# Multi-head attention by 32-row lanes in a two-layer attention and expert kernel

## The reference, cut to what matters

```python
# H = 16 heads, KPH = 4, LAT = 64, D = 128, S = 128 tokens
Q = (hs @ q_w + q_b).reshape(B, S, H, HD)     # only the first 4 of 8 columns are used
K = (hs @ k_w + k_b).reshape(B, S, H, KPH)
V = (hs @ v_w + v_b).reshape(B, S, H, KPH)
scores = einsum('bhsk,bhtk->bhst', Q[..., :KPH], K) / sqrt(KPH)
attn = softmax(scores)
ao = einsum('bhst,bhtv->bhsv', attn, V)
mla_out = concat([ao, 0]) @ o_w + o_b
# router: top 2 of 8 experts; each expert gelu(mla_out @ w1 + b1) @ w2 + b2
x = x + hs + 0.3 * moe_out                    # hs is the layer norm of x
```

## Time and profile before

| | us |
|---|---|
| median of 3 runs | 165.32 |
| lowest and highest | 164.41, 166.72 |
| the profiled execution | 164.66 |
| its span | 162.9 |

### The profile page before, as it was taken

One profiled execution on the slowest core, in us unless ns is written; L12 is line 12 of the kernel. 1 busy time (PEld: TensorE's weight loads), 2 busy tenths in 40 slices (PEclk: granted clock), 3 DMA queues, 4 the chain that ended last, 5 costly groups with the idle time before them and its releaser, 6 DMA issues.

```text
span 162.9 us, 3982 instructions
## 1 busy us (share of the span) xinstructions
PE 150.5 (92%) x1318; PEld 120.5 (74%) x1318; DVE 110.8 (68%) x408; ACT 108.3 (67%) x238; POOL 40.9 (25%) x122
## 2 busy tenths in 40 slices
PE   7998876999999999899999999999899999999891
PEld 5688755465545657457899899998799969779780
DVE  2866999879706767782228856986745897587744
ACT  8776972666785669689768743656953795666480
POOL 7698105221200294660000000220141200410100
PEclk9999997799999999999999999999999999999999
DMA  3538605217488113000100000000000000000022
GB/s 114 136 95 272 168 0 97 73 30 159 115 166 224 21 33 63 5 0 8 34 0 0 4 0 0 0 4 0 2 4 0 0 2 4 0 0 2 4 64 64
DMA packets 11071, 8.02 MB, mean 49 GB/s; under 512 B 1867, under 2 KB 10155, under 8 KB 11051
## 3 DMA queue, kind: packets, MB, share of 16 engines
q1 hardware_dynamic: 11051, 7.76, 19.5%
HBM read 5.26 MB, written 1.70 MB: 43 GB/s over the span
## 4 chain that ended last, share of the span: by engine, by line
PE 41%; issue 20%; DVE 10%; DMA 8%; ACT 7%; SPq 6%; POOL 5%; ACTq 1%; POOLq 1%; DVEq 0%
PE ps L1078 39%; DVE nmax L862 3%; DMA qbd<-scratch_q 3%; DMA w1s<-w1s 3%; DMA scratch_k<-part 2%; POOL rstd L563 2%; SPq L420 1%; ACT qbd L591 1%; SPq L371 1%; DVE qbd L856 1%; PE ps L1100 1%; POOL xn L557 1%; SPq L389 1%; ACTq L55 1%; ACT L714 1%
## 5 line engine op out<-in xcount | busy, mean ns | idle before, releaser
L699 ACT ACTIVATE vpad<-ps,b1o 128x256 f32<-128x256 f32 (+1 forms) x48 | 23.8, 545 | 16.7 <-PE ps L1078 16.6
L1078 PE MATMUL ps<-w2s,vpad 128*128 128x128 f32 x256 | 31.7, 276 | 0.2 <-DVE vpad L975 0.2
L1078 PEld LDWEIGHTS ps<-w2s,vpad 128*128 128x128 f32 x256 | 30.0, 192 | 0.8 <-issue 0.5
L862 DVE TENSOR_REDUCE nmax<-ps 128x4 f32<-128x512 f32 x32 | 21.0, 683 | 7.7 <-PE ps L1078 7.6
L975 DVE SCALAR_TENSOR_TENSOR vpad<-ps,comb,vpad 128x128 f32<-128x128 f32 x64 | 18.4, 342 | 8.6 <-PE ps L1078 8.6
L649 ACT ACTIVATE pexp<-ps 128x512 f32<-128x512 f32 x32 | 18.5, 596 | 6.1 <-PE ps L1078 5.9
L563 POOL TENSOR_TENSOR rstd<-veps,power 128x2 f32<-128x2 f32 (+1 forms) x6 | 4.8, 808 | 59.7 <-DVE veps L776 59.7
L1078 PE MATMUL ps<-ao,w_lo 128*128 128x256 f32 (+1 forms) x48 | 16.5, 358 | 0.3 <-ACT vpad L699 0.3
L1078 PE MATMUL ps<-ao,w_hi 128*128 128x256 f32 (+1 forms) x48 | 14.5, 317 | 0.0
L1078 PE MATMUL ps<-kst,qbd 128*128 128x128 bf16 x128 | 11.7, 225 | 1.4 <-DVE nmax L862 1.3
L1078 PEld LDWEIGHTS ps<-kst,qbd 128*128 128x128 bf16 x128 | 8.8, 101 | 5.7 <-issue 4.0
(11 more groups left out here) (224 smaller groups left out, 324.6 us busy)
## 6 DMA issues: line engine op xcount, KB each, us to landing
w1s<-in_L_ffn_w_dram SPq DMA_DIRECT2D x1, 1024.0 KB, 5.4
w1s<-w1s SPq DMA_DIRECT2D x8, 64.0 KB
kst<-scratch_k SPq DMA_DIRECT2D x4, 96.0 KB
qbd<-scratch_q SPq DMA_DIRECT2D x4, 96.0 KB
x<-in_x_dram SPq DMA_DIRECT2D x2, 128.0 KB, 2.4
x<-in_x_dram SPq DMA_DIRECT2D x1, 256.0 KB, 2.9
wqv<-in_L_xattn_W_qv_dram SPq DMA_DIRECT2D x1, 256.0 KB, 4.6
f1s<-in_L_ffn_W_dram SPq DMA_DIRECT2D x1, 256.0 KB, 5.0
```

Of the source, the lines that this page charges most:

```text
L699: act.activation(hT[:, k % 2, c, 0:n], ps[:, h1_bank(k, c), 0:n], ACT.Gelu, bias=b1o[:, e, c:c + 1]).then_inc(s["gelu_ok"], 1)
L862: dve.tensor_reduce(nmax[:, b, g, :], ps[:, n % 2, :].rearrange("p (j t) -> p j t", t=S), axis=AX.X, op=ALU.max, negate=True).then_inc(s[" ...
L1078: return nc.tensor.matmul(dst, lhsT, rhs, start=start, stop=stop)
```

## The change

Queries are no longer block-diagonal. `qst` holds them like the keys, one tile of [128, 4, 512] a half. A step of s1 and s2 is now a lane instead of a group: its four products contract over the 32 rows of one lane (`tile_position` (32 j, 0)), one for each group, 128 columns each. In each lane, 8 of the 32 rows are spare. The keys hold ones there, and the queries zeros. `mT` makes a second copy of the queries in PSUM (one product of 512 columns against the unit matrix) and adds to it the transposed maxima, which land in three of the spare rows; ScalarE copies this to `qm`, and s2 is then a single product a head. `selg`, its mask and the tile `mT` go. As an `av` step takes one group of all four lanes, it now needs all four exponentials of its sequence; `pexp` has seven slots.

Zeroing: `z_q` on POOL writes ones and zeros into `kst` and `qst` (4 memsets in all); `a_q` (four) and `a_k` on ScalarE go, and so do the waits for them in `parts`. `rows` makes two PSUM banks of keys, copied by ScalarE, and two of queries, copied by VectorE (2 copies instead of 16 behind ScalarE's). `gT` gets a tile of its own. The plan is a new one; FRONT stays at 2, 2 and 4.

```diff
+        qst = [sb(f"qst{i}", [P, GROUPS, T], BF16) for i in range(NHALF)]
+        qm = sb("qm", [P, 2, GROUPS, S], BF16)
+        pexp = sb("pexp", [P, SLOTS, GROUPS * S])
...
-                if h:
-                    sp.wait_ge(s["zero_q1"], GROUPS)
-                    sp.wait_ge(s["zero_k"], 1)
-                else:
-                    sp.wait_ge(s["zero_q"], u + 1)
-                    sp.wait_ge(s["qbd_ok"], GROUPS)
+                sp.wait_ge(s["zero_q"], u)
...
-                    sp.dma_start(qbd[h][rows_, :, j, d], sq).then_inc(s[f"stack_in{u}"], 16)
+                    sp.dma_start(qst[h][rows_, :, d], sq).then_inc(s[f"stack_in{u}"], 16)
...
+            def spare_rows(h):
+
+                half = slice(0 if h else T // 2, T)
+                pool.memset(kst[h][:, :, half].bitcast(FP32), PAIR_OF_ONES)
+                pool.memset(qst[h][:, :, half].bitcast(U32), 0).then_inc(s["zero_q"], 1)
...
-                for j in range(LANES):
-                    r = slice(ROWS * j, ROWS * (j + 1))
-                    last = dve.tensor_copy(qbd[0][r, g, j, 0:FRONT[0][1] * S], kst[0][r, g, T // 2:T])
-                last.then_inc(s["qbd_ok"], 1)
+                dve.wait_ge(s["rows_ps"], i + 1)
+                dve.tensor_copy(qst[0][:, 2 * i - 4:2 * i - 2, 0:T // 2],
+                                ps[:, ROW_BANKS[i], :].rearrange("p (g t) -> p g t", g=2)).then_inc(s["q0_ok"], 1)
...
-                for j in range(LANES):
-                    last = mm(ps[:, n % 2, j * S:(j + 1) * S], qbd[h][:, g, j, cols_of(b)], kst[h][:, g, cols_of(b)])
+                for g in range(GROUPS):
+                    last = mm(ps[:, n % 2, g * S:(g + 1) * S], qst[h][lane(j), g, cols_of(b)], kst[h][lane(j), g, cols_of(b)],
+                              tile=(ROWS * j, 0))
...
-                for j in range(LANES):
-                    last = mm(ps[0:MROWS, 7, j * S:(j + 1) * S], msp[:, b % 2, MROWS * j:MROWS * (j + 1)], identb[:, :])
+                mm(ps[:, 7, :].rearrange("p (g q) -> p g q", g=GROUPS), identb[:, :], qst[b // HALF][:, :, cols_of(b)], True, False)
+                for g in range(GROUPS):
+                    last = mm(ps[:, 7, g * S:(g + 1) * S], msp[:, b % 2, g, :], identb[:, :], False, g == GROUPS - 1)
...
-                mm(dst, kst[h][:, g, cols_of(b)], qbd[h][:, g, :, cols_of(b)], True, False)
-                mm(dst, selg[:, g, :], mT[:, b % 2, :, :], False, True).then_inc(s["s2_ps"], 1)
+                for g in range(GROUPS):
+                    last = mm(ps[:, 2 + n % 2, g * S:(g + 1) * S], kst[h][lane(j), g, cols_of(b)], qm[lane(j), b % 2, g, :],
+                              tile=(ROWS * j, 0))
+                last.then_inc(s["s2_ps"], 1)
...
-                pe.wait_ge(s["p_ok"], n + 1)
+                pe.wait_ge(s["p_ok"], LANES * (b + 1))
```

More of the change, by code:

```diff
@@ L1076, in _, with mm @@
         def _(pe):
-            def mm(dst, lhsT, rhs, start=True, stop=True):
-                return nc.tensor.matmul(dst, lhsT, rhs, start=start, stop=stop)
+            def mm(dst, lhsT, rhs, start=True, stop=True, tile=None):
+                return nc.tensor.matmul(dst, lhsT, rhs, start=start, stop=stop, tile_position=tile)
             def warm(n):
```

201 lines of the change are left out of this document (92 added, 109 removed).

## The result

The changed kernel takes 168.66 us (median of 4, 167.81 to 169.98), beside 164.87 us (4 runs, 164.32 to 166.72) of the kernel before on the same chip: ratio 1.022, 95% interval 1.011 to 1.033. Taken once more, beside e11, it was 169.91 us (4 runs, 168.91 to 170.59) against 165.43: 1.028, 1.021 to 1.035. By the mark of 2% the first ratio alone leaves it open whether this is slower, since its interval reaches under 1.02; the second says slower. The loss is some 4 us (3.8 and 4.5), where 165.0 and no difference had been forecast; the range, 161.2 to 169.0, holds the first median and not the second. The profiled execution took 168.47 us with a span of 166.6.

A forecast was written before the change was run, and what follows sets the result against it. TensorE was taken to bound attention's second part, behind a 13.8 us copy chain: attention to 47.9 + 27.2 = 75.1, plus expert layers 87.5 gives 162.6 of span, plus 2.4 makes 165.0 us; range 161.2 to 169.0.

The forecast's parts named there:

- rival C: TensorE's 3.2 us wait for the copies drops the clock to 1.2 GHz; 3 us lose 1.5: 166.5 us; chance 0.15.
- The front: Before sequence 4: fewer VectorE copies let the third split end at 34.1 instead of 36.2, 2.1 us gained, bounds 1.0 and 3.0.
- The copies: Third unit's chain from split to sequence 4 stays 13.8 us, start at 47.9; TensorE arrives about 44.7 and waits 3.2.
- The pace: Attention's s1 and s2 products start 0.057 us apart, 0.228 a step of four; s2 saves 6.5 us of TensorE.
- rival B: Weight loads show in s1 and s2, 0.11 us apart instead of 0.057: 172.4 us; chance 0.10.
- The overlap of neighbouring steps: Behind sequence 4's start, neighbouring steps on different rows may run side by side: at most 0.8 us, left out.
- the stretch behind sequence 4's start: From sequence 4's first product to attention's end: TensorE load 26.5 us, taken as 27.2.
- Changes of form: Attention: switching TensorE between 32-row and full products costs 0.10 us each, 36 times, 3.6 us.
- The expert layers: Same instructions in a slightly exchanged order: no change from 87.5 us, 1 us either way; any bubble after 113.
- The sum: Attention to 75.1 plus expert layers 87.5 makes 162.6 us of span; plus 2.4, 165.0 us.
- Rival A: Copies land early, second leg 2.5 us instead of 5.17, and TensorE sets the pace: 161.5 us; chance 0.25.

The follow-up runs named there:

- e11: Changed kernel with before's order in the expert layers and 53 discarded 128-row products ahead of TensorE's waits: median 170.74 us, no ratio.
- e7: e2 with its 20 discarded products cut from 128 rows to 32, same places and columns: 173.61 us, ratio 1.047.
- e2: Changed kernel with 20 discarded 128-row products at 30 to 37 us: 168.45 us, ratio 1.019.
- m1: Whole computation left out; TensorE alone runs stretches of 128-column products of 128 rows, 32 rows and both mixed, after pauses; no kernel time given.
- m2: Like m1, five more stretches: 32 rows at one or two positions, four and four mixed, some directly behind 128-row products; no kernel time given.
- e13: e12 with the changed kernel's own order in the expert layers, so the change plus discarded products: 168.32 us, ratio 1.007 from the six fastest.
- e12: e11 with 65 discarded products instead of 53: median 166.72 us over twelve executions, ratio 0.996 from the five fastest.
- e10: Changed kernel with second products' row groups in order 2, 3, 0, 1, before's order in the expert layers and 45 discarded products: 168.84 us.
- e5: Changed kernel with 79 discarded 128-row products spread over 21 to 52 us: 168.08 us (10 runs).
- e6: e5 with before's order in the expert layers: 167.53 us (4 runs).

## Why the prediction was wrong, point by point

- **The failed step is rival C's size, and with it the clock of the sum.** The prediction had the clock fall only where TensorE waits for the copies ("3 us at that clock lose 1.5: 166.5") and costed the work of the front with the durations of before, at 2.4 GHz from 30 us on. It was at 1.2 GHz from 25 to 48 us, 23 us, before any wait for the copies. Products of the form that the change brings in do this: in e7 against e2, and by themselves in m1 and m2. Of the 3.93 us that sequence 4 started after its forecast, some 2.3 go with the half clock by the rows of after: 1.40 ahead of the split and 0.93 from the landing of the copies (50.90) to TensorE's coming (51.83). I had the earlier trace rows, a low clock, and read it as one of idle time only. Had I asked what the array does in a 32-row step, nothing in the trace of before could have answered: it has none in number. That was an unknown to be bounded from both sides, like the pace. With the clock held up, e13 gives 165.27, and its line 164.8, where after has medians of 168.7 and 169.9.
- **The front.** Forecast: the third split ends at 34.1. Measured 36.76. 0.9 us are the first maximum, at 22.30 for 21.4: I took the copies' saving off the old time and forgot that TensorE's first step stands between the second copy and the maximum. 1.40 us go with the half clock in the transposes and the projection, and some 0.4 is the rest. In e12 it ended at 36.8 too, with the clock at 0.50 from 30 to 33. In e10, at full clock there, the same road from transposes to split was 3.31 us, nearly before's 3.23. Of the 2.1 us gained in the forecast, 0.8 would have been left at full clock (36.76 less 1.40, against 36.2), and e13, at full clock there, has 0.9 (35.27). So the front would have missed its forecast by over 1 us without any loss of clock.
- **The copies.** 13.8 us forecast, 13.9 measured with TensorE in time (e12). Right. TensorE was to be there at 44.7 and wait 3.2 us. At half clock it came at 51.8 and waited for none of it. With the clock mostly up it waited 0.29 us behind discarded products (e12), or came too late (e13); whether it would have waited 3.2 without them, no run shows.
- **The pace.** Products 0.057 apart, right; rival B is out. The overlap of neighbouring steps was put at 0.8 us at most and left out. Two neighbouring steps at different rows cost what one does, and the stretch behind sequence 4's start was 26.1 and 25.9 (e12) where 27.2 was forecast; so the overlap was probably larger than its bound. Changes of form at 0.1 us held.
- **The expert layers.** "Nothing, with 1 us either way", and the place named was right ("after 113"): two waits for VectorE, of 0.68 and 0.63 us. The term was put at nothing and came to 1.15 us in after. Against before's order it is about 0.9 us in the profiles, and about 1 us in time between single executions of e12 and e13.
- **The sum.** 75.1 + 87.5 came out as 77.95 + 88.65: +3.93 up to sequence 4, -1.08 behind it, +1.15 in the expert layers. That e13's line at full clock meets 165 is partly luck: the forecast had the front too early, the stretch too long by 1.3 us, the layers too short by 0.9.
- **Rival A** is out: the second leg took 5.29 us in e12 again.

Open: the slope of 1.3 to 1.5 us for 0.01 of clock holds for kernels with discarded products. For the changed kernel as it is no execution came above 0.938, so its own price of the clock is only known through e13. Open too is what makes executions of one kernel differ by over 1 us at the same mean clock, and why the clock fell in some executions of e5 and e6 before the stretch began.

## What to carry to other kernels

A cut of rows on TensorE saves no columns, and here it cost the clock. Ask what the clock will be in the new form, and not only how long the engine is busy, and bound the time of the stretch at either level before trusting its sum. Where a saving moves a chain, walk the chain's first link anew (who feeds the first instruction that it waits for?), and don't subtract from the old time. If executions of one kernel differ by some per cent, sort them by their mean granted clock before comparing medians, show all of them, and look in a trace for where the clock was lost.

## What the runs showed of the hardware that was not expected

- TensorE busy without a gap can stay at 1.2 GHz: 16.99 of 17.00 us with 32-row products at one position, and 31.85 of 32 us with four of 128 rows and four of 32 in exchange (m1). It can also fall there from 2.4 GHz with no idle time (m2).
- Nearly the same exchange of four and four stayed at 2.4 GHz for 18 us when it began there (m2): the level depends on what came before, and a kernel with mixed forms can run at either level, execution by execution (e11: 163.76 us at a mean clock of 0.996 and 173.03 at 0.930).
- 32-row products at different positions start 0.027 apart at half clock in turn over four, 0.053 in blocks at two, 0.106 at one. In the kernel this happens by itself between neighbouring steps: 0.028 apart at full clock.
- With 20 discarded 128-row products the clock came back from 0.50 to 1.00 in the midst of the kernel (e2), and with 20 of 32 rows and the same columns it did not (e7).
- The clock's row can read 1.00 at half pace at a kernel's start: in m2 it is 1.00 from 15 to 20 us, where 49 products of 128 columns start 0.10 us apart, as they do at 0.50; from 22 us on they are 0.05 apart. A mean clock leaves this stretch out, so two executions with the same mean need not have had the same clock.
